# A fused 15-phase kernel: matmuls without use in TensorE's waits, and a finer choice of experts moved ahead of the first blocks

## The reference

```
x += attention 0(layernorm x; context, 16 heads, masked by a length per item)
x += feed-forward 0: 8 experts, summed (linear, so one product matrix)
x += depool: rmsnorm, W_in, a decaying scan over the patches of the context
x += the top 15 tokens of an item: 16-head attention and a gelu feed-forward; the others pass
x += attention 2(layernorm x; context, 8 heads, masked)
x += feed-forward 2: ternary-weight linear, depthwise convolution, silu, linear
x += cross attention 3 with projections, 8 heads
x = x + MLA attention (16 heads, causal)
x = x + moe(rmsnorm x): logits = x gate_w + gate_b; top = argmax of 4 experts
        y = relu(x W1[top] + b1[top]) W2[top] + b2[top]
```

## Time and profile before

| | |
|---|---|
| runs | 1286.64, 1275.42, 1280.93 us; median 1280.93 |
| the profiled execution: its own time, its span | 1290.61 us, 1288.9 us |
| mean granted clock of TensorE over the span | 0.894 |
| busy: PE, DVE, ACT, POOL | 86%, 66%, 46%, 28% |
| phases (us from the span's start) | prep 0, L0 17.5, ffn0 203.4, depool 225.8, route 290.2, gather 311.8, L1 333.7, expand 392.1, L2 419.6, bit 541.5, cross 683.8, L3 772.9, latent 899.8, L4 959.7, experts 1177.0 |
| waits of PE over 5 us | 17.2 in route, 11.2 before L2, 11.0 before bit, 5.4 in latent, 17.6 in experts, 20.8 before L0 |

### The profile page before, as it was taken

How to read it: one execution, slowest core, us unless ns; L and a number is a source line. 1 busy time by engine, 2 the same in 40 slices (tenths; PEclk the granted TensorE clock), 3 DMA queues, 4 the chain that set the end, 5 groups by cost and what they waited for, 6 DMA issues and landing times. The chain is left out here.

```text
span 1288.9 us, 36948 instructions
## 1 busy us (share of the span) xinstructions
PE 1110.1 (86%) x13741; PEld 811.3 (63%) x13741; DVE 845.1 (66%) x2666; ACT 591.9 (46%) x1413; POOL 357.2 (28%) x899
## 2 busy tenths in 40 slices
PE   2999998892894899689997999997899999896497
PEld 2888887672453677534444557885547887775497
DVE  4677766997636588679993226886845778953333
ACT  2688864565122466512222343554763445542243
POOL 1122220122040133400000001221433665573654
PEclk9999998795797599889996897998876999986899
DMA  9600000000000000110000005000000000024373
GB/s 288 186 8 3 4 3 2 2 2 1 1 2 1 2 3 3 65 68 1 1 1 0 1 1 194 3 3 2 1 1 2 3 4 3 11 74 117 129 235 109
DMA packets 36412, 49.43 MB, mean 38 GB/s; under 512 B 8365, under 2 KB 26161, under 8 KB 35904
## 3 DMA queue, kind: packets, MB, share of 16 engines
q1 hardware_dynamic: 32480, 40.55, 10.4%
q0 software_dynamic: 2752, 6.36, 1.4%
q10 hardware_dynamic: 1008, 0.16, 0.1%
HBM read 40.71 MB, written 11.81 MB: 41 GB/s over the span
## 5 line engine op out<-in xcount | busy, mean ns | idle before, releaser
L721 PE MATMUL ps<-qTm,kT 32*128 32x512 f32 (+1 forms) x1024 | 253.9, 560 | 3.7 <-ACT probs L620 3.4
L753 PE MATMUL ps<-kT,qTm 32*128 32x128 f32 x3200 | 254.9, 295 | 0.8 <-DVE kT L425 0.8
L753 PEld LDWEIGHTS ps<-kT,qTm 32*128 32x128 f32 x3200 | 230.5, 206 | 6.1 <-issue 3.4
L524 POOL CAST nm<-neg_max 128x16 bf16<-128x16 f32 (+1 forms) x132 | 26.9, 204 | 412.1 <-DVE neg_max L384 159.4
L620 ACT ACTIVATE probs<-ps 128x1024 f32<-128x1024 f32 x72 | 73.7, 1024 | 117.1 <-PE ps L763 116.6
L912 PE MATMUL ps<-probs,v_wide 128*32 128x128 f32 x3200 | 118.7, 283 | 9.1 <-DVE ctx_all L455 4.5
L397 DVE TENSOR_REDUCE neg_max<-ps 128x8 f32<-128x1024 f32 x72 | 87.9, 1221 | 57.3 <-PE ps L753 56.2
L721 PEld LDWEIGHTS ps<-qTm,kT 32*128 32x128 f32 x1024 | 86.2, 191 | 50.8 <-issue 39.8
L392 DVE TENSOR_REDUCE neg_max<-ps 128x4 f32<-128x512 f32 x128 | 82.2, 684 | 35.7 <-PE ps L753 35.6
L616 ACT ACTIVATE probs<-ps,bias_col 128x512 f32<-128x512 f32 x128 | 80.9, 683 | 37.5 <-PE ps L763 37.5
L411 DVE TENSOR_TENSOR qTm<-ps,hmask 128x512 f32<-128x512 f32 (+1 forms) x132 | 73.3, 555 | 37.4 <-ACT nmT L598 21.0
(11 more groups left out here) (425 smaller groups left out, 2540.5 us busy)
## 6 DMA issues: line engine op xcount, KB each, us to landing
ctx_all<-in_W1T SPq DMA_DIRECT2D x38, 256.0 KB, 2.9
sorted_rows<-in_c_no_rows SPq DMA_DIRECT2D x1, 4940.0 KB, 20.8
kv_all<-sorted_rows SPq DMA_DIRECT2D x38, 130.0 KB, 2.6
ctx_all<-in_ctx SPq DMA_DIRECT2D x4, 1024.0 KB, 10.4
ctx_all<-in_ctxT SPq DMA_DIRECT2D x2, 2048.0 KB, 10.1
x_all<-in_x SPq DMA_DIRECT2D x4, 512.0 KB, 7.0
tap_w<-in_conv_wT SPq DMA_DIRECT2D x1, 768.0 KB, 6.6
out<-q_all,kv_all POOLq DMA_INDIRECT x38, 3.3
```

Source lines behind the costliest of these rows:

```text
L721: nc.tensor.matmul(ps[:, bank, at:at + N], kT[rows_of(g), k, :], qTm[rows_of(g), k, 0:N], start=True, stop=False, skip_group_check=True)
L753: last = nc.tensor.matmul(dst, qTm[rows_of(g), k, 128 * i:128 * i + 128], kT[rows_of(g), k, :], start=False, stop=True, skip_group_check=True)
```

## The change

TensorE gets matmuls whose result nothing reads, at the start of each phase but after the barrier, and inside the first five items of every attention:

```diff
+        FILL = 5
+
+        def keep_busy(pe, spot, count=1):
+
+            wide = spot.shape[1]
+            for _ in range(count):
+                nc.tensor.matmul(spot, identb[:], sel_max[:].rearrange("p i q -> p (i q)")[:, 0:wide], start=True, stop=True,
+                                 skip_group_check=True)
+
+        def keep_busy_early(pe):
+
+            pe.wait_ge(sem("ones_set"), 1)
+            for _ in range(44):
+                nc.tensor.matmul(ps[:, 0, 0:128], ones[:], ones[:], start=True, stop=True)
...
                             bank, at = raw_at(L, b, g, N)
+                            if b < FILL:
+                                keep_busy(pe, ps[:, bank, at:at + N], 512 // N)
...
                     raw_free(b, a)
+                    if b < FILL:
+                        keep_busy(pe, ps[:, raw_bank(L, b, a), :])
...
+            keep_busy(pe, ps[:, 0, :], {"L0": 16, "L1": 14, "L2": 48, "L3": 8, "L4": 8}[L])
             whole_steps(pe, count, TURN_LAG[post], step)
...
         def route_tensor(pe):
+            keep_busy(pe, ps[:, 7, :], 64)
             pe.wait_ge(sem("rt_wcol"), 1)
             nc.tensor.matmul(ps[0:B, 4, 0:128], wcol[:], ident[:], start=True, stop=True).then_inc(sem("rt_wT"), 1)
+            keep_busy(pe, ps[:, 7, :], 11)
...
         def bit_tensor(pe):
+            keep_busy(pe, ps[:, 7, :], 46)
...
         def cross_tensor(pe):
+            keep_busy(pe, ps[:, 7, :], 16)
...
             pe.wait_ge(sem("la_raw"), B)
+            keep_busy(pe, ps[:, 7, :], 20)
...
         def expert_tensor(pe):
+            keep_busy(pe, ps[:, 7, :], 14)
...
-            dict(sync=prep_sync, scalar=prep_scalar, gpsimd=prep_gpsimd, vector=prep_vector),
+            dict(sync=prep_sync, scalar=prep_scalar, gpsimd=prep_gpsimd, vector=prep_vector, tensor=keep_busy_early),
```

The choice of experts loses the Sqrt on ScalarE, and is cut into 15 pieces:

```diff
-CHOICES = 6
+CHOICES = 5
...
-        CHOICE_STEPS = (HALF + 7, HALF + 8, HALF + 9, HALF + 12, HALF + 13)
-        RANK_STEPS = (HALF + 11, HALF + 12, HALF + 15, HALF + 16)
-        NORM_STEPS = tuple(range(HALF + 9, HALF + 13))
-        SEND_STEP = HALF + 13
+        CHOICE_STEPS = tuple(HALF + 7 + i for i in (0, 1, 2, 3, 4, 5, 6, 9, 10, 11, 12))
+        RANK_STEPS = (HALF + 15, HALF + 16, HALF + 20, HALF + 21)
+        NORM_STEPS = tuple(range(HALF + 12, HALF + 16))
+        SEND_STEP = HALF + 18
...
                 if at_step(items) >= SEND_STEP:
-                    for b in itertools.islice(rows, 2):
+                    for b in itertools.islice(rows, 2 if at_step(items) < B + 2 else 3):
                         send_row(pool, b)
...
+            yield
+            q(V.tensor_scalar(inv.bitcast(I32), var.bitcast(I32), -0.5, HALF_POWER, ALU.mult, ALU.add))
+            for newton in range(3):
+                if newton:
+                    yield
+                q(V.scalar_tensor_tensor(part, var, -0.5, inv, ALU.mult, ALU.mult))
+                q(V.tensor_tensor(part, part, inv, ALU.mult))
+                q(V.scalar_tensor_tensor(inv, part, 1.5, inv, ALU.add, ALU.mult))
             dve.sem_inc(sem("so_choice"), 1)
             yield
-            dve.wait_ge(sem("so_root"), g + 1)
-            q(V.reciprocal(inv, moment[:, 5, 0:HALF]))
...
-        def take_root(act, g):
-
-            act.wait_ge(sem("so_choice"), CHOICES * g + 1)
-            nc.scalar.activation(moment[:, 5, 0:HALF], moment[:, 1, 0:HALF], ACT.Sqrt).then_inc(sem("so_root"), 1)
```

In experts seven pieces of the second half's choice come before any block, the rest earlier than before, and blocks 0 to 2 take all four relus on ScalarE:

```diff
-        RANK_BLOCKS = (4, 5, 8, 9)
+        RANK_BLOCKS = (1, 1, 4, 4)
+        ALL_RELU = 3
...
             def add(j):
                 dve.wait_ge(sem("bk_down"), j + 1)
-                if j in RANK_BLOCKS:
+                for _ in range(RANK_BLOCKS.count(j)):
                     next(chain)
...
+            for _ in range(7):
+                next(chain)
+            norm_late(0)
             for t in range(BLOCKS + 1):
...
-                if t in (0, 1, 2, 6, 7):
+                if t in (2, 4):
+                    next(chain)
                     next(chain)
-                if 2 <= t < 6:
-                    norm_late(t - 2)
+                if t == 2:
+                    for part in range(1, 4):
+                        norm_late(part)
...
-                for c in (0, 1):
-                    nc.scalar.activation(hidden3[:, j % 2, 128 * c:128 * c + 128], hidden_at(j, c),
-                                         ACT.Relu, bias=block_bias[:, c, j:j + 1]).then_inc(sem("bk_relu_early"), 1)
-            table_for(act, ACT.Sqrt)
+                for c in range(4 if j < ALL_RELU else 2):
+                    if c == 2:
+                        act.wait_ge(sem("bk_up"), 2 * j + 2)
+                    nc.scalar.activation(hidden3[:, j % 2, 128 * c:128 * c + 128], hidden_at(j, c), ACT.Relu,
+                                         bias=block_bias[:, c, j:j + 1]).then_inc(sem("bk_relu_early"), 1)
             for t in range(BLOCKS + 1):
-                if t == 1:
-                    take_root(act, 1)
```

More of the change, by code:

```diff
@@ L31 @@
 MAGIC = 12582912.0
+HALF_POWER = float(0x5F3759DF)
 LOWEST = -3.4028234663852886e38
@@ L656, in step @@
                     norm_rows(act, NORM_STEPS.index(at_step(items)))
-                if L == "L4" and at_step(items) == CHOICE_STEPS[0]:
-                    take_root(act, 0)
             table_for(act, ACT.Exp)
@@ L793, in mask_whole @@
                     raw_free(b, 2 + a)
+                    if b < FILL:
+                        keep_busy(pe, ps[:, raw_bank(L, b, 2 + a), :])
                 if cut_later:
@@ L851, in first_part @@
                     if L == "L4" and at_one + 1 in RANK_STEPS:
-                        rank_part(pe, 0, RANK_STEPS.index(at_one + 1), ps[:, 6, 448:512])
+                        last = rank_part(pe, 0, RANK_STEPS.index(at_one + 1), ps[:, 6, 448:512])
                     if item(1):
@@ L1091, in ffn0_tensor @@
         def ffn0_tensor(pe):
+            keep_busy(pe, ps[:, 7, :], 8)
             def multiply(b, k):
@@ L1316, in gather_tensor @@
         def gather_tensor(pe):
+            keep_busy(pe, ps[:, 7, :], 9)
             pe.wait_ge(sem("ga_pick"), 1)
@@ L1857, in build @@
         WIDE = N_EXP3 * HALF
-        RANK_BLOCKS = (4, 5, 8, 9)
+        RANK_BLOCKS = (1, 1, 4, 4)
+        ALL_RELU = 3
         def rank_spot(g, part):
-            return ps[:, 3 + RANK_BLOCKS[part] % 2, 128:256] if g else ps[:, 6, 448:512]
+            at = 128 + 64 * (part % 2)
+            return ps[:, 3 + RANK_BLOCKS[part] % 2, at:at + 64] if g else ps[:, 6, 448:512]
         def rank_part(pe, g, part, spot):
@@ L1867, in rank_part @@
             if part < 2:
[L1868 to L1871, removed]
+                pe.wait_ge(sem("so_choice"), CHOICES * g + 2)
+                return nc.tensor.matmul(spot[:, 0:WIDE], (onesb, upperb)[part][:], chosen, start=True, stop=True)
+            pe.wait_ge(sem("so_choice"), CHOICES * g + 4)
             for i in range(2):
                 c = 2 * (part - 2) + i
-                nc.tensor.matmul(spot[:, HALF_BLOCKS * i:HALF_BLOCKS * (i + 1)], b12_parts[:, 128 * c:128 * c + 128],
-                                 block_hot[:, blocks_of(g)], start=True, stop=True)
+                last = nc.tensor.matmul(spot[:, HALF_BLOCKS * i:HALF_BLOCKS * (i + 1)], b12_parts[:, 128 * c:128 * c + 128],
+                                        block_hot[:, blocks_of(g)], start=True, stop=True)
+            return last
         def choice(dve, g):
@@ L1973, in send_row @@
                 pool.wait_ge(sem("experts_loaded"), 32)
-                pool.wait_ge(sem("so_choice"), 4)
+                pool.wait_ge(sem("so_choice"), 3)
             if b == HALF:
                 pool.wait_ge(sem("so_scattered"), 16 * HALF)
-                pool.wait_ge(sem("so_choice"), CHOICES + 4)
-                pool.wait_ge(sem("so_rows"), HALF + 4)
-            if b < HALF:
-                pool.wait_ge(sem("so_rows"), b + 1)
+                pool.wait_ge(sem("so_choice"), CHOICES + 3)
+            pool.wait_ge(sem("so_rows"), b + 1 if b < HALF else HALF + (b - HALF) // 4 + 1)
             pool.wait_ge(sem("so_joined"), 2 * (b + 1))
@@ L1995, in split_expert_biases, with relu_done @@
             q(V.tensor_copy(b12_parts[rows, :], b12[rows, :]))
+        def relu_done(engine, j):
+            engine.wait_ge(sem("bk_relu_early"), 2 * (j + 1) + 2 * min(j + 1, ALL_RELU))
+            if j >= ALL_RELU:
+                engine.wait_ge(sem("bk_relu_late"), 2 * (j + 1 - ALL_RELU))
         def stored(j):
@@ L2011, in relu @@
             def relu(j):
+                if j < ALL_RELU:
+                    return
                 dve.wait_ge(sem("bk_up"), 2 * j + 2)
@@ L2099, in down @@
             def down(j, start):
-                pe.wait_ge(sem("bk_relu_early"), 2 * (j + 1))
-                pe.wait_ge(sem("bk_relu_late"), 2 * (j + 1))
+                relu_done(pe, j)
                 if j >= 2:
                     pe.wait_ge(sem("bk_added"), j - 1)
-                if j in RANK_BLOCKS:
```

(5 more changed lines are left out.)

20 lines of the change are left out of this document (9 added, 11 removed).

## The result

The changed kernel takes 1317.96 us (median, 1310.38 to 1319.12) against 1278.18 for the kernel before on the same chips: a ratio of 1.0292, interval [1.0244, 1.0339], so 2.9% slower. I had said 1264, with 0.15 for slower. The profiled execution took 1317.48, its span is 1315.8.

The account below looks back on a forecast made before the run. TensorE was taken to bound most phases, often at half clock after waits. Terms 32.1 - 12.4 - 5.5 + 3 = 17.2 us saved took the profiled 1290.61 to 1273.4, on the median's scale 1264; range 1253 to 1271.

Parts of the forecast that it names:

- the price of an inner filler: Attentions, first five items: 0.22 us per filler at full clock, 0.44 at half; 4.4 us per attention where TensorE bounds.
- L0's and L2's returns: Early items at full clock: L0 11.2 less 4.4, +6.8; L2 7.7 less 4.4, its turn 9.7 late, -6.4.
- Cross: Start of cross: seven items at 2.27 us in place of 4.0, fillers 0.4 too long: 11.7 us saved.
- ffn0, depool and gather together: These phases: half of the 10.1 us ceiling from half-clock work comes back, 5 us saved.
- the 12 us that bit's fillers take: Start of bit: 46 fillers take 12.7 us in 9.46 of wait, 3.3 late; 2 us lost in all.
- L1 and latent: L1: 14 fillers cost 3.9 us ahead of useful work, 4 lost; latent: three quarters of 6.3 back, 4.7 saved.
- L4's tail: End of L4: last send 3.7 us later, SyncE's 6.48 us of loads following; 5.5 us lost (3 to 9).
- Experts: Experts: Sqrt's wait and GpSimd's 2.81 us go, clock returns 2, fillers cost 3.9: 3 us saved (-2 to +6).
- The slower rival: At barriers of L2, bit, L1, L4, experts, cross: fillers run at half clock, 9 to 36 us slower, 1303; chance 0.15.
- the marks of being wrong: Cross or L4 still starting at half clock behind their fillers, or L4's row loads coming no later than its attention.
- the signs: Among them: L0's turns 273 ns from the first, L2's turn 13 us behind its barrier, L4's last send about 4 later.
- The first rival: Experts: TensorE's stall goes too as sends overlap the blocks, 17.6 us more saved, 1246; chance 0.08.

Follow-up runs that it names:

- the kernel with bunched fillers: The changed kernel with the two inner fillers of a score-group pair together ahead of the pair in L0, L2 and L3: ratio 1.0079 to the kernel before.
- the fitted kernel: The changed kernel with only fillers that fit a wait behind the barrier (none inside attentions, prep, L0, L1, expand, experts; fewer in L2, bit): 1268.22 us, ratio 0.9899.
- the choice alone: The changed kernel with no filler at all, the finer and earlier choice of experts kept: ratio 1.0003 to the kernel before.

## Why the prediction was wrong

**The step that failed** is the price of an inner filler: "4 x 5 x 0.22 = 4.4 us per attention, paid where TensorE is the bound". I priced a filler as its own streaming time, and took the matmuls around it to go on as they were. In L1, L2, L3 and L4 that is near what the kernel without inner fillers gives back (4.1, 4.7, 6.4, 3.3 us); in L0 it is 25.4, and all together are 42.6 us of span. A filler of 128 rows between two groups of 32 breaks a pair that runs side by side, and keeps the softmax scores apart from both; in L0 this came at half clock, where one filler cost 1.73 us, and the half clock lasted 51 us. The rows that spoke against my price stood in the trace of before, L721 beside L746: I read L859's pace there and not its neighbours.

**L0's and L2's returns** failed with it. L0 had +6.8 and lost 27.3. It was at half clock for 17 us or more wherever that was recorded, but for the kernel with bunched fillers, and that one gained nothing by it (188.8): early steps with fillers at full clock are as long as early steps without at half. In L2 the turn came 9.4 us late (I had 9.7), but 7.7 less 4.4 of return was -2.6.

**Cross**, -11.7, measured -12.0 in the two traces, is right by them and wrong as a forecast: four of six traces of kernels without fillers do not have that loss. The 9.7 us between the profiled execution and the median, which I named, were mostly this: the next profile of the kernel before is 13.4 us shorter, and 11.9 of them are cross. A return that is read from a profile at the far end of the runs is not the return at the median.

**Right within 2 us**: ffn0, depool and gather together, and the 12 us that bit's fillers take (12.1 from the barrier to the first turn; I had 12.7), though bit became 1.1 shorter and not 2 longer. L1 and latent are right by number alone. L1's fillers at its start cost 2.7 us (58.4 against 55.7), its inner ones 4.1, and 2.7 came back; I had 3.9 and set the rest off. Latent has the same 56 us in the two kernels with the new choice and no filler, so its 3.5 are not shown to be the fillers' return.

**L4's tail** was forecast nearly right, in part by luck. The last send was to end 3.7 us later, counted from the turn at 1088.1; it ended 83.3 us behind that turn (1110.5 in the changed kernel) where it had been 80.7, 2.6 later. But counted from zero, as the code counts its steps, that turn is step 23 and not 24, so I had step 34 one step too early; and I let TensorE's steps behind item 31 go on at 5.45 us, where they hold less and are shorter. The two cancel: the first send came 57.0 us behind the turn, I had 57.3. From the first send on, 26.3 us for sends, cuts and joins were as worked out (27.1). L4's start gave back 5.9 us net (3.9 forecast), and so the last send came 3.3 us earlier counted from L4's start, where I had named 4 later as a sign. The rows of L4 in the changed kernel:

```profile
L2017 POOL DMA_INDIRECT sorted_rows<-kv_all,slot_i x15: 967/978/1007, 1169.0 to 1192.8; - x15
...
1195.36 6.84 SPq L2200 DMA_DIRECT2D kv_all<-sorted_rows  x12
...
1202.83 4.51 PE L1030 MATMUL ps<-sel_max,identb 128*128 128x512 bf16 x13 [16.00 <-SPq L1043]
```

That GpSimd's sends and SyncE's loads, not attention, end L4 was right: TensorE waits 16.00 us there.

**Experts**, +3 forecast, lost 1.6: its fillers took 4.5 us in front of the first block (I had 3.9). The pause of 2.81 us ahead of the first send went (0.30), but the last of the five stores started 24.3 us behind the barrier, 20.1 before. In the fitted kernel, which lacks these fillers, it starts at 20.9, and with the choice alone at 21.3: most of the delay is the fillers', and the pieces moved ahead made that store about 1 us later, not earlier.

The slower rival named the barrier and L2 as its place. Its mechanism, fillers at half clock ahead of useful work, is a part of the loss (L2's overrun, and 3.2 us in experts); the larger part was in no rival. What I had named as the marks of being wrong did not come: behind their fillers cross and L4 run at full clock in this trace, and L4's row loads end after its attention. Of the signs, L0's turns (up to 474 ns) and L4's last send failed; none of them measured a filler's price. (The first rival's time is 1246 by its sum; the 1244 in the range is a slip.)

## What to carry to other kernels

Price an added matmul by what it stands between: where neighbours run side by side on parts of the array, a full-width one costs their overlap, and perhaps the clock: 25.4 us for twenty fillers in L0, where their own time is 4.4. Fill a wait only with what fits behind the barrier that opens it, and check how far the profiled execution stands from the median before a slow stretch in it is counted as a return. A higher mean clock is no gain by itself, 0.940 here with 40 us more; and a transfer queue's order (weights behind rows that wait for something else) gave 9 us for one loop.

## What the runs showed of the hardware

- The same kernel comes to a phase at either clock: cross at half clock for 34 us in one execution of the kernel before, for 10 us in two others, with the same instructions. PE was busy 31.10 of 31.10 us of the slow one, so work without a gap did not end it at once.
- The recorded clock missed L0's half clock in the trace of before (1.00 with turns of 474 ns) and had it in the changed kernel's, where TensorE had worked in prep (half from 31.7 to 82.9, turns up to 474). All traces go this way: the window of L0 has 0.99 or less in the five with fillers in prep, and 1.00 in the nine without, whose first turns last up to 474 ns too.
